# A two-layer gated cross-attention kernel: the key weights' split, the third norm's order, and matmul fillers in the router

## What is computed

```python
x = x + tanh(g_xattn[0]) * attention0(norm(x), ctx)   # 32 heads, 8 key heads, rotary
x = x + tanh(g_ffn[0])   * (norm(x) @ W.T + bias)      # W dequantized, 512 x 512
x = x + tanh(g_xattn[1]) * attention1(norm(x), ctx)   # one head of width 512: Q = xn Wq + bq, K = ctx Wk + bk
x = x + tanh(g_ffn[1])   * experts(norm(x))            # router over 32 experts, best 2 of each token
```

## Time and profile before

| | us |
|---|---|
| median of 3 runs | 922.22 (921.65 to 926.31) |
| the profiled execution, device time | 924.77 |
| its span in the profile | 923.0 |
| PE busy | 842.6 (91%) |
| DVE busy | 660.6 (72%) |
| POOL busy | 426.9 (46%) |
| ACT busy | 393.8 (43%) |

### The profile page before, as it was taken

One profiled execution on the slowest core, in us unless ns is written; L12 is line 12 of the kernel. 1 busy time (PEld: TensorE's weight loads), 2 busy tenths in 40 slices (PEclk: granted clock), 3 DMA queues, 4 the chain that ended last, 5 costly groups with the idle time before them and its releaser, 6 DMA issues. The chain is left out here.

```text
span 923.0 us, 13113 instructions
## 1 busy us (share of the span) xinstructions
PE 842.6 (91%) x4337; PEld 705.8 (76%) x4337; DVE 660.6 (72%) x1303; ACT 393.8 (43%) x1005; POOL 426.9 (46%) x386
## 2 busy tenths in 40 slices
PE   5688899999999999999999999987989999989980
PEld 4576788888888888888888888866878687777860
DVE  3947588876778786787786778775463557999974
ACT  4334334423424433433533432443223446878970
POOL 5459626643634833643842643512020048875730
PEclk9979999999999999999999999998999968999995
DMA  8301200300110200110110120004200466999817
GB/s 333 150 1 46 98 17 1 114 1 1 48 68 1 103 11 0 45 69 1 57 57 0 45 91 1 1 1 186 105 1 12 177 234 198 366 344 340 314 36 274
DMA packets 23641, 91.13 MB, mean 99 GB/s; under 512 B 6576, under 2 KB 7088, under 8 KB 15776
## 3 DMA queue, kind: packets, MB, share of 16 engines
q1 hardware_dynamic: 17440, 81.00, 23.9%
q0 software_dynamic: 6144, 9.46, 2.9%
HBM read 86.23 MB, written 14.68 MB: 109 GB/s over the span
## 5 line engine op out<-in xcount | busy, mean ns | idle before, releaser
L359 POOL TENSOR_TENSOR qT<-straight,turned 128x512 f32<-128x512 f32 x64 | 82.5, 1289 | 154.7 <-DVE turned L557 154.2
L455 ACT ACTIVATE probs<-bank,negmax 128x128 f32<-128x128 f32 x256 | 90.5, 366 | 134.5 <-DVE negmax L568 134.5
L557 DVE TENSOR_TENSOR turned<-bank,sinT 64x512 f32<-64x512 f32 x160 | 110.2, 689 | 2.2
L133 PE MATMUL bank<-wo_hi,oT_hi 128*128 128x512 f32 x256 | 100.9, 394 | 8.7 <-DVE oT_lo L581 6.2
L133 PE MATMUL bank<-xT_hi,wq_hi 128*128 128x512 f32 x256 | 105.3, 411 | 2.1 <-DVE xT_lo L109 2.0
L135 PE MATMUL bank<-xT_hi,wq_lo 128*128 128x512 f32 x256 | 100.6, 393 | 0.0
L134 PE MATMUL bank<-xT_lo,wq_hi 128*128 128x512 f32 x256 | 100.4, 392 | 0.0
L135 PE MATMUL bank<-wo_hi,oT_lo 128*128 128x512 f32 x256 | 99.8, 390 | 0.0
L134 PE MATMUL bank<-wo_lo,oT_hi 128*128 128x512 f32 x256 | 99.8, 390 | 0.0
L462 ACT ACTIVATE pT_hi<-bank 128x512 fp32r<-128x512 f32 x64 | 38.3, 599 | 130.9 <-PE bank L722 130.9
L555 DVE TENSOR_TENSOR straight<-bank,cosT 128x512 f32<-128x512 f32 x80 | 55.3, 691 | 46.0 <-PE bank L135 45.4
(11 more groups left out here) (226 smaller groups left out, 2108.4 us busy)
## 6 DMA issues: line engine op xcount, KB each, us to landing
ring<-in_ew SPq DMA_DIRECT2D x28, 1024.0 KB, 8.4
raw_big<-in_wq SPq DMA_DIRECT2D x8, 1024.0 KB, 4.8
raw_big<-in_wo SPq DMA_DIRECT2D x8, 1024.0 KB, 4.8
early_w<-in_ew SPq DMA_DIRECT2D x8, 1024.0 KB, 8.5
ring<-picked SPq DMA_DIRECT2D x8, 512.0 KB, 7.3
raw_k<-in_wk SPq DMA_DIRECT2D x8, 256.0 KB, 5.0
ctx_raw<-in_ctxT SPq DMA_DIRECT2D x4, 512.0 KB, 6.0
raw_v<-in_wv SPq DMA_DIRECT2D x8, 256.0 KB, 5.0
```

The costliest lines, as they stand in the source:

```text
L133: nc.tensor.matmul(out_, hi, r_hi, start=start, stop=False)
L359: nc.gpsimd.tensor_tensor(dst, straight[:, k, :], turned[:, k, :], ALU.add).then_inc(rope_sum, 1)
L455: ex = nc.scalar.activation(probs[:, u % 2, h, :], bank_scores[u % 2][:, h * S:(h + 1) * S], ACT.Exp, bias=negmax[:, u % UNITS, h:h + 1], ...
L557: last = nc.vector.tensor_tensor(turned[dst, k, :], bank[src, :], sinT[src, tok], ALU.mult)
```

## The change

POOL's split of the key weights goes to DVE, ahead of the norm's reciprocal, and ACT makes two chunks of `w_hi` before its root and two behind it. The third norm's root on ACT goes ahead of the query weights' upper parts, its four tiles are applied in a row, turned in a row on banks 0 to 3 between forward 4 and forward 5, and their rests stand behind `add_forward(4)`. The router's laps get three fillers each, on bank 6, with a wait for `g_added` at 7 ahead of the loop in place of 8 behind it; three more stand between the last `rank` and `codes`, and the last fill has 18 in place of 16.

```diff
 def ln_bank(n, t):
-    return psum[t % 2 if n else 4 + t % 2]
+    return psum[t if n == 2 and t < 4 else t % 2 if n else 4 + t % 2]
...
 def norm_turn(pe, n, t, xn):
     pe.wait_ge(ln_norm, n * NB + t + 1)
-    if n * NB + t >= 2:
+    if n == 2 and t in (2, 3):
+        pe.wait_ge(g_kept, 2 * KC)
+    elif n * NB + t >= 2:
         pe.wait_ge(ln_lo, n * NB + t - 1)
...
 # POOL
-    weights_rest(0)
-    weights_rest(1)
+    for c in range(KC):
+        pool.wait_ge(g_whi, KC + c + 1)
+        nc.gpsimd.tensor_tensor(w_lo[:, :, columns(c)], w_raw[1][:, :, columns(c)],
+                                w_hi[:, :, columns(c)].bitcast(F32), ALU.subtract).then_inc(g_wlo, 1)
...
 # ACT
+    weights_upper(0, range(2))
     norm_sqrt(act, 3, HALVES[1])
-    weights_upper(0)
+    weights_upper(0, range(2, KC))
...
     for i in range(2, 2 * KC):
         keep(i)
-    weights_upper(1)
     norm_sqrt(act, 4, HALVES[0])
     for t in HALVES[0]:
         norm_upper(act, 2, t)
+    weights_upper(1, range(KC))
     keep(8)
...
 # DVE
-    norm_stats(dve, 1, 3, HALVES[1])
+    def key_rest(chunks):
+        for c in chunks:
+            dve.wait_ge(g_whi, c + 1)
+            nc.vector.tensor_tensor(w_lo[:, :, columns(c)], w_raw[0][:, :, columns(c)],
+                                    w_hi[:, :, columns(c)].bitcast(F32), ALU.subtract).then_inc(g_wlo, 1)
+    norm_spread(dve, 1, HALVES[1])
+    key_rest(range(2))
+    norm_rstd(dve, 3, HALVES[1])
+    key_rest(range(2, KC))
...
     norm_stats(dve, 2, 4, HALVES[0])
-    norm_apply(dve, 2, 0, last_xn)
-    norm_apply(dve, 2, 1, last_xn)
+    for t in HALVES[0]:
+        norm_apply(dve, 2, t, last_xn)
     add_forward(4)
-    norm_apply(dve, 2, 2, last_xn)
-    norm_apply(dve, 2, 3, last_xn)
-    norm_rest(dve, 2, 0)
+    for t in HALVES[0]:
+        norm_rest(dve, 2, t)
     add_forward(5)
-    norm_rest(dve, 2, 1)
-    norm_rest(dve, 2, 2)
     add_forward(6)
-    norm_rest(dve, 2, 3)
     add_forward(7)
...
 # PE
     forward(4)
+    for t in HALVES[0]:
+        norm_turn(pe, 2, t, last_xn)
     forward(5)
-    norm_turn(pe, 2, 0, last_xn)
-    norm_turn(pe, 2, 1, last_xn)
     forward(6)
-    norm_turn(pe, 2, 2, last_xn)
-    norm_turn(pe, 2, 3, last_xn)
     forward(7)
...
     router_turn(3)
+    pe.wait_ge(g_added, NB - 1)
     for t in range(2, NB):
         logits(t)
         if t + 2 < NB:
             router_turn(t + 2)
         rank(t - 1)
+        fill(6, 3)
         codes(t - 2)
-    pe.wait_ge(g_added, NB)
     rank(NB - 1)
+    fill(6, 1)
     codes(NB - 2)
+    fill(6, 2)
     codes(NB - 1)
     count_all()
-    fill(6, 16)
+    fill(6, 18)
```

More of the change, by code:

```diff
@@ L1097, in _, with weights_upper @@
             def _(act):
-                def weights_upper(w):
+                def weights_upper(w, chunks):
                     act.wait_ge(g_in[w], 16)
@@ L1101, in weights_upper @@
                         act.wait_ge(g_mm, 2 * KC)
-                    for c in range(KC):
+                    for c in chunks:
                         nc.scalar.activation(w_hi[:, :, columns(c)], w_raw[w][:, :, columns(c)], ACT.Copy).then_inc(g_whi, 1)
```

## The result

Median 919.7 us (916.7 to 921.1, 8 runs) against 924.9 for the kernel before on the same chip (921.7 to 927.0, 8 runs): ratio 0.9945, 95% interval 0.9928 to 0.9962. That is 5.2 us, or 0.55%, faster. The forecast was 7.4 us, to 914.8. The saving was overrated by 2.2 us; the rest of the distance to 914.8 is the base: the three runs that it started from had a median of 922.22, and all later sets of the kernel before 924.8 to 925.6. As a ratio the forecast was 0.992, just outside the interval. The profiled execution took 918.04 us, span 916.3, mean granted clock 0.972 (before 924.77, 923.0, 0.958).

What follows compares the result with a forecast made beforehand. PE was busy 91% of the span, so time was to be won only where it idled or ran at its lower clock; savings of 1.9, 3.3 and 2.2 made 7.4 us, from 922.22 to 914.8, range 911.8 to 918.8.

Steps and rivals of the forecast that it cites:

- Part 1: Block start, key weights: PE's first matmul 1.38 us earlier plus some clock; 1.9 us saved, bounds 1.4 and 3.5.
- Part 2: Third norm: PE's idle waits and half clock between forward 4 and project 8 shrink; 3.3 us saved, bounds 2.7 and 4.3.
- half-clock stretch that I discounted: Third norm, forward 7 at half clock: 1.6 us of the possible 4.3, counted only partly because typical runs lose less clock.
- The rival of a moved stall: Third norm: forward 7 or project 8 waits 2.4 us instead, giving 917.2, or 919.4 with no router gain; chance 0.07.
- Part 3: Router: fillers hold the full clock through the laps; 2.2 us saved, bounds 0 and 2.6.
- The rule that the prediction set against this: Router: clock stays up without long idle gaps between matmul bursts, so fillers only cost; covered by a rival of chance 0.08.
- The rival "router gains nothing": Router: cross-engine chains hold the laps and fillers eat what is won; only 5.2 us saved, to 917.0; chance 0.17.
- The step that failed: Behind the slot table: only the table's gain counts, POOL's queue moves as one, expert weights and row stores follow semaphores.

Runs made afterwards that it cites:

- keys_only: Kernel before with only the key weights' change (split on DVE, ACT's root behind two copies); ratio to the kernel before 1.0017 (0.9997 to 1.0037).
- keys_hold: Kernel before with only the key weights' change, plus SP's ring loads held until the first eight gathers have landed; ratio to the kernel before 1.0030 (1.0014 to 1.0046).
- norm_only: Kernel before with only the third norm's change (root first, four tiles on four banks); ratio to the kernel before 0.9969 (0.9949 to 0.9988).
- fill_only: Kernel before with only the router's fillers added; ratio to the kernel before 0.9984 (0.9970 to 0.9998).
- no_fill: Changed kernel without the router's fillers, keeping the key weights' and third norm's changes; ratio to the kernel before 0.9956 (0.9934 to 0.9978).
- after_again: The changed kernel measured once more, with nothing altered; median 920.82 us, ratio to the kernel before 0.9933 (0.9908 to 0.9957).
- after_hold: Changed kernel with SP's ring loads held until the first eight gathers have landed; ratio to the kernel before 0.9973 (0.9949 to 0.9997).
- mix: Changed kernel with POOL's queue reordered: gathers 0 to 4, combine weights, then gathers and scatters in turn; median 914.94 us, ratio to the kernel before 0.9886.

## Why the prediction was off

**Part 1: the term was right.** First matmul 1.40 us earlier (forecast 1.38), 1.86 at the scores in keys_only (forecast 1.9). But keys_hold, the same kernel up to there, has 0.88: the clock fell at the block start in both, as expected, for 6.8 us in keys_hold as before the change and for 3.4 in keys_only. So the size of this term hangs on how long the fall lasts.

**Part 2: right, and larger.** 4.5 us from forward 4 to project 8, 4.7 at the scores in norm_only, where the forecast took 3.3 between 2.7 and 4.3: the half-clock stretch that I discounted went as a whole. The ground for that discount was wrong: the profiled execution (924.77) was no slow one, it was at the median of the later sets. The rival of a moved stall was wrong: no wait on `xT_lo` in this stretch.

**Part 3: right to the table.** 3.1 us from the scores to the last count in fill_only, over the forecast's 2.2 and its bound of 2.6. Beside parts 1 and 2 it was less: the changed kernel is 1.6 us ahead of no_fill there (50.46 against 52.03) and 1.9 at the last count; laps of 2.43 and 2.04 where 2.5 and 2.1 stood, and logits 4 to the last codes in 10.9, not 11.6. The fillers hold the clock mostly, not always: in the seven profiles without them it fell in the router each time, 102.5 to 113.2 us from the barrier and for 17.1 to 27.3 us; in the seven with them five show no fall up to the last count, after_again one at 114.9 for 10.2 us and fill_only one at 123.4 for 6.8. The rule that the prediction set against this (the Trainium skill, "TensorE: Matmul & The Clock Gate", "Why this matters for your kernels") did not hold here: keys_only, without fillers, ran 17.1 us of its router at a clock of 0.50 with PE busy for 16.43 of them. The rival "router gains nothing" fell at the table. Its price at the end, 5.2 us for parts 1 and 2 alone, is what was measured, but by another mechanism: that is luck.

**The step that failed** is the one behind the table: "So of PE's earlier freedom only the table's counts, and POOL's queue moves as one", and with it "After that nothing is tied to absolute time". Three things were wrong in it. PE's freedom did count: with the closing fillers at full clock it reached slot 2 10.67 us earlier, where the table was only 8.7 earlier. POOL's queue did not move as one: earlier slots brought DVE's splits onto the casts and the subtraction, +1.79 us between take 1 and take 2. And the gather's flight is not a constant: 4.68 us in the changed kernel with a load just ahead, 3.33 in after_hold with none. Before the change PE waited 0.47 us for this gather; that this was a margin of nearly nothing, with a queue behind it that gains less than PE does, could be read in the trace and was not priced. In its place stood a wait of 5.60 us. The scatters were the next wall, also in the earlier trace rows. That this step cost the missing us is shown by mix: with POOL's order mended the same change gives 10.6 us, and the same order without the change gives nothing. How much of it is the gather's wall and how much the scatter's was not separated.

The range was too narrow for the same reason. It took bounds from the three terms and none from what the earlier work runs into, and it started from a median of three runs that lay 2.7 us under that of eight.

What stays open: why the clock fell at slots 12 and 18 in the first profile of the changed kernel (3.4 us each, at about 1.7 us of time, which together are about the 3.5 us lost between results 11 and 18) when it did so once each in norm_only, fill_only and no_fill, and never there in the ten other profiles. PE had just waited 2.1 and 2.0 us for DVE's `xT_lo` at the two places, but it waited as long in after_again, 2.07 and 2.00, and the clock held. No run was made on it. That a typical run of the changed kernel has the gather wait is likely by the estimate above, and not shown.

## What to carry to other kernels

When a change makes a stage earlier, list every queue that feeds the next stage and ask of each whether it gains as much as the engine that consumes it; a wait of 0.47 us on the old trace is a queue with no slack, and the difference in gains becomes the new wait. Price the repair together with the change: an order that was free before may be worth as much as the change after it (here 0 and 5.9 us), and the parts timed alone may not show it (2.8 us in sum, 5.2 together, 10.6 with the queue mended). On a software queue, put what the next consumer wants ahead of bulk work, and interleave takes with gives instead of filling all buffers first.

## What the runs showed of the hardware

- The granted clock fell to 0.50 straight after 6.80 us in which PE was never idle, and stayed there for 6.80 us more, mostly of gapless 96x512 matmuls (fill_only). Router laps of small matmuls ran at half clock for 17 to 27 us with PE busy for 96% to 98% of it; three 96x512 matmuls in each lap kept the clock at 1.00 up to the last count in five profiles of seven.
- POOL's cast pair and subtraction of 128x256 took 0.74 and 0.73 us alone and 1.62 and 1.64 beside DVE's subtraction of two SBUF tiles of 128x1024.
- A gather of a slot's rows landed 3.3 us after its issue at best. With 1 MB loads just ahead it took 4.68, 6.51 and 6.59 us; the same gathers with the loads held back took 3.33, 4.26 and 4.74, the last two behind an issuing instruction of 1.93 us in place of 1.08.
- The same program's unchanged first block varied by 3.9 us between profiled executions, as much as a part of this change is worth; times from a common barrier were needed to see anything.
